# Three attention layers on one core: the order of the first projections, the queue of the next layer's weights, and the order of GpSimd's norm

## The chip, the cores and the metric

One core of a Trainium2 chip runs the whole program. The metric is the device time in microseconds (us); of three runs of the kernel before the median is 2946.81 us (2944.68 to 2946.95).

## The reference, cut to what matters

x has 32 sequences of 128 positions and 512 features. Four layers follow each other, each added to x. The change touches the first three, and the preparation in front of them.

```python
def _L0(x, cond, ...):     # attention, 16 heads of 32 features
    q, k, v = x @ Wqkv.T + bqkv
    attn = softmax(q @ k.T / sqrt(32))
    coh = sigmoid(tanh(concat(x, cond) @ Wc1.T + bc1) @ Wc2.T + bc2)
    mod = attn * coh
    mod = mod / (mod.sum(-1) + 1e-8)
    out = ((1 - 0.21) * mod + 0.21 * fa) @ v      # fa: one row of weights per sequence
    return out @ Wout.T + bout

def _L1(x, mask, cond, ...):
    attn = softmax(where(mask, -inf, q @ k.T * scale))
    out = (attn @ v) @ Wo.T
    return out / rms(out) * rms_scale * (1 + sc) + shift

def _L2(x, t, ...):
    x = x + attention(g1 * x / rms(x) + b1)
    return x + swiglu(g2 * x / rms(x) + b2)       # hidden width 2048

x = x + _L0(x); x = x + _L1(x); x = x + _L2(x); x = x + _L3(x)
```

## The kernel before, in words

The program has three phases, with a barrier of all engines between them: `prepare` (small vectors, and the first weights), `attention` (the attention of three layers), and `gated_mlp`. The change is in the first two.

**Exact products.** Every matrix product in fp32 is made of three passes: an operand is split into a high part (a copy in fp32r by ScalarE, L104, L1013) and a low part (the difference, by VectorE or GpSimd, L109, L1218, L1334). `mm3` then multiplies high by high, high by low and low by high. So before a weight or x can be used it must be loaded, made high, and made low. `Splitter` does that for a list of loads through a few staging tiles: a load waits until the low part of the load that last used its tile is done.

**The start.** `prepare` splits the whole tiles of k's and q's weights of layer 0 (L104 on ScalarE, L109 on VectorE) at its end, and loads the first x and the two halves of c's weights ahead. `attention` then begins with the split of x (`high_x(0)`, `low_x(0)`), and splits the halves of c, v and o. A prologue projects the first group in the order c, v, k, q (c is the projection inside the tanh).

**Bodies.** There are 48 bodies, 16 for each layer; a body handles a group of two sequences. In it are eight units (u = 0 to 7, four heads of one sequence). A unit goes: scores on TensorE (L797), maximum and difference on VectorE (L1129, L1133), exponential on ScalarE (L964), high part on ScalarE (L959), low part on VectorE (`low_probs`, L1137, both inputs in SBUF), a transposition by DMA (`turn_probs`, L652, issued by SyncE), and the weighing of the values on TensorE (`weigh_values`, L813). Between them TensorE makes the projections of the next group (L746 to L748 in two PSUM banks `bank_a`), whose results ScalarE and VectorE read (L947 or L949, L1122), and turns the outputs (L845). `iterate` runs every layer's first body and last three written out, and the twelve between as a loop. Each engine does its own instructions strictly in the order of the code; `pieces_of` sets in which of twelve slots of a body each half of a projection falls.

**Queues.** SyncE issues every transfer: eight transposes per body, and between them a store of the last group's result, loads of residual and x, in some bodies a piece of the weights of later layers (loaded, split and stored in DRAM as `split_h`, `split_l`). At the borders of the layers, `swap` loads the split weights of the next layer back (L684, `new_weight`, 16 transfers of 512 KB per border): four at the end of body 14 (30), eight in body 15 (31), one behind each unit's transposition, and four in and behind the last units of body 16 (32). It waits for the last use of the tile that is written over. The order on SyncE is:

```python
for u in range(UNITS):
    turn_probs(i, u)
    if u == 0 and piece_of(i) is not None:
        load_piece(piece_of(i))
    swap(i, u)
```

**GpSimd.** Values are split into three bf16 parts: `first_values` on ScalarE (L993), `rest_of_values` on GpSimd (L1341), `second_values` on ScalarE (L997), `third_values` on GpSimd (L1345). In layer 2 the norm of x two groups ahead ends on GpSimd too (`norm_end`, eight operations, L1358), behind everything else of the body, when VectorE has scaled x (L1201). In layer 1 `norm_add` (L1211, eight operations of VectorE with two inputs in SBUF) adds the normed output.

**The query mask.** In layer 1, `normalise` multiplies the reciprocal sums (128x8) by `any_key` (L1151) and then the weighed values by the result (L1159).

Of the kernel before, what the change touches and what calls it, by code (L numbers as in the profile page):

```python
# [115 lines left out]
def prepare(nc, hold, k, a, weights, ahead):  # L116

    with ExitStack() as ctx:
# [35 lines left out]
        ws = Splitter(nc, hold, "prep", weights, [sb(f"stage{n}", [P, CH * E]) for n in range(2)])  # L154
# [13 lines left out]
        def _(sp):  # L168
# [7 lines left out]
            for dst, src in ahead:  # L176
                sp.dma_start(dst, src).then_inc(ahead_loaded, 16)
            sp.wait_ge(ahead_loaded, 16 * len(ahead))
# [48 lines left out]
        def _(act):  # L227
# [13 lines left out]
            for n in range(len(weights)):  # L241
                ws.high(act, n)

# [112 lines left out]
def attention(nc, hold, k, x_in, x_out, wh, wl, a, split_h, split_l, hh, hl, xin, spare, stored):  # L356
# [5 lines left out]
    with ExitStack() as ctx:  # L362
# [35 lines left out]
        with ExitStack() as first_layer:  # L398
# [106 lines left out]
        def a_turn(p, fill):  # L505
# [6 lines left out]
            place = 1 if kind == "o" else 2 if kind == "c" else 3 + c - early if kind == "v" else 0 if m == 1 else 2 + c + early  # L512
# [84 lines left out]
        def z_turn(i, j):  # L597

            return 2 * (4 * i + j) if lay(i) < 2 else 4 * i + j + 4 * 2 * G
# [20 lines left out]
        def _(sp):  # L620
# [42 lines left out]
            for n in range(ws.staged, FIRST):  # L663
# [17 lines left out]
            def new_weight(layer, n, m, part):  # L681
                p = len(PIECES) * (layer - 1) + PIECES.index((n, m))
                t, w = ((split_h, wh), (split_l, wl))[part]
                sp.dma_start(f32(columns(w[n], m)), t[p].rearrange("p (c e) -> p c e", c=CH)).then_inc(new_weights[n, m], 16)  # L684

            def last_use(layer, kind, m):
                bk, _ = a_turn(G * layer - 1, (kind, m))
                sp.wait_ge(a_full[bk], a_done(G * layer - 1, (kind, m)))

            def swap(i, u):  # L690

                for layer in (1, 2):
                    at = i - G * layer if isinstance(i, int) else None
                    if at == -2 and u == UNITS:
                        sp.wait_ge(piece_stored, 32 * len(PIECES) * layer)
                        for n in "kq":
                            last_use(layer, n, 0)
                            for part in range(2):
                                new_weight(layer, n, 0, part)
                    if at == -1 and u < 4:  # L700
                        if u == 0:
                            last_use(layer, "v", 1)
                        new_weight(layer, "v", u // 2, u % 2)
                    if at == -1 and 4 <= u < UNITS:
                        if u == 4:
                            last_use(layer, "q", 1)
                        new_weight(layer, "kq"[u // 2 - 2], 1, u % 2)
                    if at == 0 and u >= UNITS - 2:
                        if u == UNITS - 2:
                            last_use(layer, "o", 1)  # L710
                        for m, part in ([(0, u - UNITS + 2)] if u < UNITS else [(1, 0), (1, 1)]):
                            new_weight(layer, "o", m, part)

# [616 lines left out]
        def _(pool):  # L1330
# [38 lines left out]
            def body(i):  # L1369
# [10 lines left out]
                if pre(i):  # L1380
                    norm_end(i + 2)
# [529 lines left out]
```

## Time and profile before

| | |
|---|---|
| Median of three runs | 2946.81 us |
| Time of the profiled execution | 2946.95 us |
| Its span | 2945.2 us |
| TensorE busy | 2832.9 us, 96% |
| VectorE busy | 2077.9 us, 71% |
| ScalarE busy | 1386.7 us, 47% |
| GpSimd busy | 672.8 us, 23% |
| Preparation and prologue | until about 70 us |
| Layers 0, 1, 2 | about 70 to 720, to 1300, to 1856 us |

The span runs from the first instruction to the last; the time has a little around it. Busy time counts no waiting on semaphores, but an instruction that stands inside an engine counts as busy. The row of a timeline gives start, duration, engine, line, and in brackets how long the engine was idle before it and what ended that. "PEclk" is the clock granted to TensorE: 1.00 is its high level (2.4 GHz), 0.50 its low one (1.2 GHz).

### The profile page before, as it was taken

The numbers are of one execution on the slowest core, as the hardware profiler recorded it, in microseconds if no ns is written. First come the engines' busy times: TensorE is split into PE (matmuls) and PEld (weight loads), VectorE is DVE, ScalarE is ACT, GpSimd is POOL, SyncE is SP. The second block draws the span as 40 slices with busy tenths as digits, with TensorE's granted clock in tenths as the row PEclk, the third lists the DMA queues.
The fourth block names the chain that finished last, engine by engine and source line by source line (L and its number), as shares of the span: only waits on it lengthen the run. The fifth ranks groups of instructions, "written<-read, shape, count | busy, mean of one in ns | idle before, by whom it ended". The sixth has DMA issues, their size and how long they took to land. (4 is left out here: it accounts for less than half of the span.)

```text
span 2945.2 us, 69390 instructions
## 1 busy us (share of the span) xinstructions
PE 2832.9 (96%) x26999; PEld 2488.1 (84%) x26999; DVE 2077.9 (71%) x3640; ACT 1386.7 (47%) x2254; POOL 672.8 (23%) x563
## 2 busy tenths in 40 slices
PE   6999999998999999988999998999999999999997
PEld 5899999998899999888888887788888888888886
DVE  5777777786799999978888888644444465555554
ACT  3555555554566666656666666322222232222221
POOL 1222222221111121133233322222222221111112
PEclk8999999999999999999999999999999999999999
DMA  3554544457544443575434445321122230111101
GB/s 141 105 133 117 134 131 136 128 122 187 133 112 105 110 111 100 126 176 135 109 103 115 106 114 128 129 69 60 57 71 84 90 98 29 58 44 51 48 29 43
DMA packets 514586, 300.44 MB, mean 102 GB/s; under 512 B 411776, under 2 KB 484608, under 8 KB 513952
## 3 DMA queue, kind: packets, MB, share of 16 engines
q1 hardware_dynamic: 514464, 298.76, 37.9%
q8 instruction: 83, 1.36, 0.2%
q14 instruction: 39, 0.32, 0.0%
HBM read 139.31 MB, written 58.72 MB: 67 GB/s over the span
## 5 line engine op out<-in xcount | busy, mean ns | idle before, releaser
L746 PE MATMUL att_bank_a<-keep_hh,keep_wgateh 128*128 128x256 f32 x1536 | 449.3, 293 | 0.9 <-ACT att_af L915 0.9
L964 ACT ACTIVATE att_shifted<-att_shifted,keep_lift 128x512 f32<-128x512 f32 x384 | 276.2, 719 | 341.2 <-DVE att_shifted L1133 341.2
L747 PE MATMUL att_bank_a<-keep_hh,keep_wgatel 128*128 128x256 f32 x1536 | 435.3, 283 | 0.0
L748 PE MATMUL att_bank_a<-keep_hl,keep_wgateh 128*128 128x256 f32 x1536 | 435.1, 283 | 0.0
L1730 DVE TENSOR_TENSOR mlp_act_t<-mlp_bank_u,mlp_sg 128x512 f32<-128x512 f32 x128 | 88.4, 690 | 453.5 <-ACT mlp_sg L1636 449.8
L1636 ACT ACTIVATE mlp_sg<-mlp_bank_g 128x512 f32<-128x512 f32 x128 | 76.7, 599 | 628.9 <-PE mlp_bank_u L1560 628.9
L1779 POOL TENSOR_TENSOR mlp_al<-mlp_act_t,mlp_ah 128x512 fp32r<-128x512 f32 x128 | 174.7, 1365 | 863.0 <-ACT mlp_ah L1642 863.0
L1137 DVE TENSOR_TENSOR att_pq<-att_shifted,att_pq 128x512 f16<-128x512 f32 x384 | 331.2, 865 | 45.2 <-ACT att_pq L959 42.6
L746 PEld LDWEIGHTS att_bank_a<-keep_hh,keep_wgateh 128*128 128x128 f32 x1536 | 294.6, 192 | 4.4 <-ACT att_af L915 1.1
L747 PEld LDWEIGHTS att_bank_a<-keep_hh,keep_wgatel 128*128 128x128 f32 x1536 | 295.1, 192 | 0.1
L748 PEld LDWEIGHTS att_bank_a<-keep_hl,keep_wgateh 128*128 128x128 f32 x1536 | 295.0, 192 | 0.0
L1129 DVE TENSOR_REDUCE att_top<-att_bank_s 128x4 f32<-128x512 f32 x384 | 261.2, 680 | 32.7 <-PE att_bank_s L797 32.6
L1133 DVE TENSOR_TENSOR att_shifted<-att_bank_s,att_top 128x512 f32<-128x512 f32 x384 | 265.5, 691 | 16.4
L959 ACT ACTIVATE att_pq<-att_shifted 128x512 f16<-128x512 f32 x384 | 242.4, 631 | 66.6 <-DMA att_pt<-att_pq 47.2
L813 PEld LDWEIGHTS att_bank_o<-keep_v,att_pt 128*128 128x128 f16 x7680 | 206.4, 96 | 59.4 <-DVE att_of L1159 19.5
L813 PE MATMUL att_bank_o<-keep_v,att_pt 128*128 128x34 bf16 x7680 | 226.9, 178 | 28.7 <-DMA att_pt<-att_pq 17.5
L746 PE MATMUL att_bank_a<-att_oth,keep_wuph 128*128 128x256 f32 x768 | 225.9, 294 | 20.4 <-DVE att_kl L1122 17.5
L747 PE MATMUL att_bank_a<-att_oth,keep_wupl 128*128 128x256 f32 x768 | 217.2, 283 | 0.0
L748 PE MATMUL att_bank_a<-att_otl,keep_wuph 128*128 128x256 f32 x768 | 217.0, 283 | 0.0
L1560 PE MATMUL mlp_bank_y<-mlp_al,mlp_woh 128*128 128x512 f32 x512 | 203.5, 398 | 0.0
L1558 PE MATMUL mlp_bank_y<-mlp_ah,mlp_woh 128*128 128x512 f32 x512 | 202.2, 395 | 1.4 <-POOL mlp_al L1779 1.4
L1559 PE MATMUL mlp_bank_y<-mlp_ah,mlp_wol 128*128 128x512 f32 x512 | 202.9, 396 | 0.0
(268 smaller groups left out, 7123.0 us busy)
## 6 DMA issues: line engine op xcount, KB each, us to landing
resid<-att_xres SPq DMA_DIRECT2D x47, 512.0 KB, 3.0
keep_xin<-resid SPq DMA_DIRECT2D x33, 512.0 KB, 3.8
mlp_res<-resid SPq DMA_DIRECT2D x32, 512.0 KB, 4.5
att_xres<-resid SPq DMA_DIRECT2D x31, 512.0 KB, 4.1
mlp_xf<-resid SPq DMA_DIRECT2D x30, 512.0 KB, 4.5
keep_xin<-in_x SPq DMA_DIRECT2D x16, 512.0 KB, 4.2
att_xres<-in_x SPq DMA_DIRECT2D x16, 512.0 KB, 3.9
keep_spare<-in_w_next SPq DMA_DIRECT2D x16, 512.0 KB, 3.8
```

The source lines that it names most:

```text
L746: nc.tensor.matmul(out, w_h, x_h, start=first, stop=False)
L747: nc.tensor.matmul(out, w_l, x_h, start=False, stop=False)
L748: return nc.tensor.matmul(out, w_h, x_l, start=False, stop=last)
L813: mm = nc.tensor.matmul(bank_o[:, o:o + VW], pt[:, u % TURNED, part, h, :], v[:, b, 4 * c + h, :], start=(n == 0), stop=(n == len(passes) ...
L959: nc.scalar.activation(pq[:, u % 2, 0], shifted[:, u % 2], ACT.Copy).then_inc(p_high, 1)
L964: nc.scalar.activation(shifted[:, u % 2], shifted[:, u % 2], ACT.Exp, bias=k["lift"][:, 0:1], scale=SCALE).then_inc(exp_done, 1)
L1129: nc.vector.reduce_max(top[:, u % 2, :], src, AX_X).then_inc(top_ready, 1)
L1133: nc.vector.tensor_tensor(shifted[:, u % 2], src, bcast_last(top[:, u % 2, :], P), ALU.subtract).then_inc(shift_done, 1)
L1137: nc.vector.tensor_tensor(pq[:, u % 2, 1], shifted[:, u % 2], pq[:, u % 2, 0], ALU.subtract).then_inc(p_low, 1)
L1558: nc.tensor.matmul(out, w[0], x_h, start=first, stop=False)
L1559: nc.tensor.matmul(out, w[1], x_h, start=False, stop=False)
L1560: return nc.tensor.matmul(out, w[0], x_l, start=False, stop=last)
```

## The change

1. `prepare` splits only v's weights (one load, one staging tile). It also splits the first x: high part on ScalarE behind v's, low part on GpSimd (a wait for `x_loaded`, one for `x_high`). `attention` no longer does either.
2. The prologue projects v, then c, k, q. Eight half-tile loads (c, k, q, o) go through the three staging tiles; their splits stand at given slots of the prologue (`SPLIT_AT`), among the reads of the results, the last (o) before q's read.
3. `new_weight`, `last_use` and `swap` move from SyncE to ScalarE, unchanged in themselves; ScalarE calls `swap` for two units at the end of each pair of units.
4. SyncE issues two transposes, then what else belongs to the pair: the piece's load stands behind unit 1 (before: 0), the store behind unit 5 (before: 4), the residual and x loads where they were.
5. GpSimd does `norm_end` in the next body, between `rest_of_values` and `third_values` (before: last in the body before). The final one stands behind all bodies.
6. In layer 1 the factor `any_key` is part of the operation at L1159; L1151 and a wait go.

```diff
-        ws = Splitter(nc, hold, "prep", weights, [sb(f"stage{n}", [P, CH * E]) for n in range(2)])
+        ws = Splitter(nc, hold, "prep", weights, [sb("stage", [P, CH * E])])
...
         @block.gpsimd
...
+            high, low = x_split
+            pool.wait_ge(x_high, 1)
+            nc.gpsimd.tensor_tensor(low, ahead[0][0], f32(high), ALU.subtract)
...
             for n in range(len(weights)):
                 ws.high(act, n)
+            act.wait_ge(x_loaded, 16)
+            nc.scalar.activation(x_split[0], ahead[0][0], ACT.Copy).then_inc(x_high, 1)
...
-        FIRST = 6
+        SPLIT_AT = {0: (0, 1), 7: (2, 3), 8: (4, 5), 10: (6, 7)}
...
-                 for n in "cvo" for m, part in enumerate(halves)]
+                 for n in "ckqo" for m, part in enumerate(halves)]
...
-            ahead = values + keys if values_first(i) else keys + values
-            return [("k", 1), ("q", 1), ("o", 0), ("o", 1)] + ([("c", 0), ("c", 1)] if lay(i + 1) == 0 else []) + ahead
+            hidden = [("c", 0), ("c", 1)] if lay(i + 1) == 0 else []
+            return [("k", 1), ("q", 1), ("o", 0), ("o", 1)] + (values + hidden + keys if values_first(i) else hidden + keys + values)
...
             def body(i):
-                for u in range(UNITS):
+                for u in range(0, UNITS, 2):
                     turn_probs(i, u)
+                    turn_probs(i, u + 1)
                     if u == 0 and piece_of(i) is not None:
                         load_piece(piece_of(i))
-                    swap(i, u)
-                    if u == 1 and post(i):
+                    if u == 0 and post(i):
                         load_residual(i - 1)
                     if u == 4 and positive(i) and not post(i):
                         store(i - 1)
-                    if u == 5 and has(i, 2) and lay(i + 2) < 2:
+                    if u == 4 and has(i, 2) and lay(i + 2) < 2:
                         load(i + 2)
...
-                swap(i, UNITS)
...
         @block.scalar
...
+            def new_weight(layer, n, m, part):
+                p = len(PIECES) * (layer - 1) + PIECES.index((n, m))
+                t, w = ((split_h, wh), (split_l, wl))[part]
+                act.dma_start(f32(columns(w[n], m)), t[p].rearrange("p (c e) -> p c e", c=CH)).then_inc(new_weights[n, m], 16)
...
             act.wait_ge(eps_set, 1)
-            high_x(0)
             for s, pieces in enumerate(pieces_of(-1)):
-                if s < FIRST and s % 2 == 0:
-                    for n in (s, s + 1):
-                        ws.high(act, n)
+                for n in SPLIT_AT.get(s, ()):
+                    ws.high(act, n)
...
+                    if s < UNITS:
+                        swap(i, s)
+                        swap(i, s + 1)
+                swap(i, UNITS)
...
-                if lay(i) == 1:
-                    nc.vector.tensor_scalar(r, r, k["any_key"][:, 0:1], None, ALU.mult).then_inc(rz_step, 1)
...
-                nc.vector.tensor_tensor(dst, src[:, :, :, 0:HD], scale, ALU.mult).then_inc(o_free, 1)
+                if lay(i) == 1:
+                    nc.vector.scalar_tensor_tensor(out=dst, in0=src[:, :, :, 0:HD], scalar=k["any_key"][:, 0:1], in1=scale,
+                                                   op0=ALU.mult, op1=ALU.mult).then_inc(o_free, 1)
+                else:
+                    nc.vector.tensor_tensor(dst, src[:, :, :, 0:HD], scale, ALU.mult).then_inc(o_free, 1)
...
             def body(i):
                 for b in range(NB):
                     rest_of_values(i, b)
+                if positive(i) and pre(i - 1):
+                    norm_end(i + 1)
                 for b in range(NB):
                     third_values(i, b)
...
-                if pre(i):
-                    norm_end(i + 2)
 
             iterate(pool, body)
+            norm_end(ALL + 1)
             low_x(ALL + 1)
...
-            early = [(a["L0_" + n], flat3(wh[n]), flat3(wl[n])) for n in "kq"]
+            early = [(a["L0_v"], flat3(wh["v"]), flat3(wl["v"]))]
...
-            phase(prepare, a, early, ahead)
+            phase(prepare, a, early, ahead, (hh[:, :, 0:T], hl[:, :, 0:T]))
```

## Rows read from the trace of the kernel before

**Rows 1.** The page, part 1: busy time, share of the span, instructions

```profile
PE 2832.9 (96%) x26999; PEld 2488.1 (84%) x26999; DVE 2077.9 (71%) x3640; ACT 1386.7 (47%) x2254; POOL 672.8 (23%) x563
```

**Rows 2.** TensorE's waits, total, times, longest: 60-690, 695-800, 1184-1375, 1375-1753 us

```profile
PE att_bank_s L797 <- DVE att_shifted L1133: 4.9, 1, 4.9
...
PE att_bank_o L813 <- DMA att_pt<-att_pq: 9.5, 6, 4.4
...
PE att_bank_o L813 <- DMA att_pt<-att_pq: 5.3, 4, 1.9
...
PE att_bank_a L746 <- DVE att_kl L1122: 10.8, 12, 0.9
```

**Rows 3.** Layer 1: busy PE, PEld, DVE, ACT, POOL, then clock, DMA, GB/s

```profile
801.00:1184.00 383.00, 381.47 (x4999) 348.61 (x4998) 352.41 (x635) 257.64 (x402) 80.08 (x57) 1.00 0.42 107
```

**Rows 4.** The timeline of the start

```profile
32.50 4.48 DVE L109 TENSOR_TENSOR keep_wgatel<-prep_stage,keep_wgateh 128x2048 fp32r<-128x2048 f32 x2
...
38.01 1.06 ACT L1013 ACTIVATE keep_hh<-keep_xin 128x1024 fp32r<-128x1024 f32 x1 [6.71 <-DVE att_eps L1224]
...
42.73 0.58 PE L746 MATMUL att_bank_a<-keep_hh,att_wch 128*128 128x256 f32 x1 [11.85 <-DVE att_wcl L109]
...
54.08 0.50 PE L746 MATMUL att_bank_a<-keep_wuph,keep_hh 128*128 128x512 f32 x1 [3.14 <-ACT att_tf L933]
...
70.95 0.69 DVE L1129 TENSOR_REDUCE att_top<-att_bank_s 128x4 f32<-128x512 f32 x1 [1.96 <-PE att_bank_s L797]
```

**Rows 5.** The start in windows, columns as in rows 3

```profile
44.00:46.00 2.00, 2.00 (x11) 2.00 (x11) 0.00 (x0) 0.64 (x1) 0.00 (x0) 0.50 0.92 330
...
54.00:60.00 6.00, 5.92 (x19) 4.73 (x20) 0.94 (x2) 2.32 (x7) 2.56 (x2) 0.72 0.00 0
...
64.00:66.00 2.00, 2.00 (x19) 2.00 (x18) 0.76 (x2) 0.84 (x2) 0.00 (x0) 1.00 0.00 0
```

**Rows 6.** Borders: timeline, windows, and lines 652 (1240-1310 us) and 684 (680-724)

```profile
703.41 1.72 SPq L652 DMA_TRANSPOSE att_pt<-att_pq  x1
...
708.93 0.75 PE L813 MATMUL att_bank_o<-keep_v,att_pt 128*128 128x34 bf16 x20 [4.38 <-DMA att_pt<-att_pq]
...
706.00:708.00 2.00, 0.00 (x0) 0.00 (x0) 0.00 (x0) 0.00 (x0) 0.00 (x0) 0.67 1.13 278
...
680.00:723.00 43.00, 36.94 (x446) 33.56 (x445) 26.65 (x58) 17.20 (x31) 4.87 (x4) 0.92 0.71 185
...
L652 SPq DMA_TRANSPOSE att_pt<-att_pq x11: 1232/1819/3964, 1242.6 to 1306.2; - x11
...
DMA to landing us min/median/max: 2.7/4.7/8.1
...
L684 SPq DMA_DIRECT2D keep_wgateh<-split_h x2: 583/584/585, 701.6 to 708.4; - x2
```

**Rows 7.** The start of a body of layer 2: timeline, and the body's window

```profile
1544.24 3.45 POOL L1358 TENSOR_SCALAR att_xf<-att_xf,att_gt,att_bt 128x128 f32<-128x128 f32 x8 [22.33 <-DVE att_xf L1201]
1547.66 2.22 POOL L1341 TENSOR_TENSOR att_vr<-att_vf,keep_v 128x512 f32<-128x512 f32 x2
...
1547.58 2.84 DVE L1137 TENSOR_TENSOR att_pq<-att_shifted,att_pq 128x512 f16<-128x512 f32 x1 [0.22 <-ACT att_pq L959]
...
1551.75 0.38 PE L746 MATMUL att_bank_a<-att_oth,keep_wuph 128*128 128x256 f32 x1 [0.94 <-DVE att_kl L1122]
...
1517.30:1550.80 33.50, 32.38 (x438) 29.73 (x434) 29.50 (x47) 21.77 (x36) 10.65 (x14) 1.00 0.42 110
```

**Rows 8.** Line 1211 beside the norm's end (second border), and alone (layer 1)

```profile
1298.97 4.21 POOL L1358 TENSOR_SCALAR att_xf<-att_xf,att_gt,att_bt 128x128 f32<-128x128 f32 x8 [9.64 <-DVE att_xf L1201]
...
1299.28 2.30 DVE L1211 SCALAR_TENSOR_TENSOR att_xres<-att_af,att_gt,att_xres 128x128 f32<-128x128 f32 x8
...
868.04 2.18 DVE L1211 SCALAR_TENSOR_TENSOR att_xres<-att_af,att_gt,att_xres 128x128 f32<-128x128 f32 x8
```

**Rows 9.** The costliest groups of VectorE: busy, mean ns, idle before

```profile
L1151 DVE TENSOR_SCALAR att_rz<-att_rz,keep_any_key 128x8 f32<-128x8 f32 x64 | 33.0, 515 | 2.3
```

More of the change, by code:

```diff
@@ L113, in flat3, with prepare @@
     return t[:].rearrange("p c e -> p (c e)")
-def prepare(nc, hold, k, a, weights, ahead):
+def prepare(nc, hold, k, a, weights, ahead, x_split):
     with ExitStack() as ctx:
@@ L175, in _ @@
                 ws.load(sp, n)
-            for dst, src in ahead:
+            x, x_dram = ahead[0]
+            sp.dma_start(x, x_dram).then_inc(x_loaded, 16)
+            for dst, src in ahead[1:]:
                 sp.dma_start(dst, src).then_inc(ahead_loaded, 16)
-            sp.wait_ge(ahead_loaded, 16 * len(ahead))
+            sp.wait_ge(ahead_loaded, 16 * (len(ahead) - 1))
         @block.gpsimd
@@ L662, in _ @@
             sp.sem_inc(x_loaded, 16)
-            for n in range(ws.staged, FIRST):
+            sp.sem_inc(x_high, 1)
+            sp.sem_inc(x_split, 1)
+            for n in range(ws.staged, len(loads)):
                 if n == 4:
@@ L1019, in high_piece, with last_use, swap @@
                 nc.scalar.activation(part_h[:], spare[0][:], ACT.Copy).then_inc(piece_high, 1)
+            def new_weight(layer, n, m, part):
+                p = len(PIECES) * (layer - 1) + PIECES.index((n, m))
+                t, w = ((split_h, wh), (split_l, wl))[part]
+                act.dma_start(f32(columns(w[n], m)), t[p].rearrange("p (c e) -> p c e", c=CH)).then_inc(new_weights[n, m], 16)
+            def last_use(layer, kind, m):
+                bk, _ = a_turn(G * layer - 1, (kind, m))
+                act.wait_ge(a_full[bk], a_done(G * layer - 1, (kind, m)))
+            def swap(i, u):
+                for layer in (1, 2):
+                    at = i - G * layer if isinstance(i, int) else None
+                    if at == -2 and u == UNITS:
+                        act.wait_ge(piece_stored, 32 * len(PIECES) * layer)
+                        for n in "kq":
+                            last_use(layer, n, 0)
+                            for part in range(2):
+                                new_weight(layer, n, 0, part)
+                    if at == -1 and u < 4:
+                        if u == 0:
+                            last_use(layer, "v", 1)
+                        new_weight(layer, "v", u // 2, u % 2)
+                    if at == -1 and 4 <= u < UNITS:
+                        if u == 4:
+                            last_use(layer, "q", 1)
+                        new_weight(layer, "kq"[u // 2 - 2], 1, u % 2)
+                    if at == 0 and u >= UNITS - 2:
+                        if u == UNITS - 2:
+                            last_use(layer, "o", 1)
+                        for m, part in ([(0, u - UNITS + 2)] if u < UNITS else [(1, 0), (1, 1)]):
+                            new_weight(layer, "o", m, part)
             act.wait_ge(eps_set, 1)
-            high_x(0)
             for s, pieces in enumerate(pieces_of(-1)):
-                if s < FIRST and s % 2 == 0:
-                    for n in (s, s + 1):
-                        ws.high(act, n)
+                for n in SPLIT_AT.get(s, ()):
+                    ws.high(act, n)
                 for fill, part in pieces:
@@ L1224, in _ @@
             nc.vector.memset(eps[:], 1e-6).then_inc(eps_set, 1)
-            low_x(0)
             nc.vector.tensor_copy(tb[:], k["tanh_bias"][:, :, 0:NB]).then_inc(tb_ready, 1)
             for s, pieces in enumerate(pieces_of(-1)):
-                if s < FIRST and s % 2 == 0:
-                    for n in (s, s + 1):
-                        ws.low(dve, n)
+                for n in SPLIT_AT.get(s, ()):
+                    ws.low(dve, n)
                 for fill, part in pieces:
```

45 lines of the change are left out of this document (8 added, 37 removed).

## The prediction

> **What bounds the kernel now.** I read the page first: TensorE is busy 96% of the span, no other engine over 71% [rows 1]. So an edit pays only where it takes away an idle stretch of TensorE, or a stretch at its half clock. The second view is TensorE's waits, stage by stage [rows 2]: after the start there is one wait of 4.9 us in the 630 us of layer 0, and in the middle of layer 1 TensorE is busy 381.5 of 383 us [rows 3]. Nothing is to be won there. What is left lies in four places: the start, the two borders of the layers, and one wait of some 0.9 us in every body of layer 2.
>
> The sum is made against the profiled execution, 2946.95 us (span 2945.2); the median of the runs shown is 2946.81, the same for this purpose. About 0.2% (5.9 us) can be told from no change here.
>
> **The change, part by part.**
>
> *1. The start.* The timeline shows the chain [rows 4]. In the preparation VectorE splits two full weight tiles (k, q) in 4.48 us, 2.24 each, until 36.98. ScalarE's next work starts at 38.01, 1.03 later: the border of the phases. Then the first x is split and c's two halves, and only at 42.73 does TensorE start, having waited 11.85 us. The change leaves one tile (v) in the preparation, moves x's split there (its low part from VectorE to GpSimd), and lets TensorE start with v. Preparation ends at 32.50 + 2.24 = 34.74, and I add 0.5 us because GpSimd now works beside VectorE at its end (below); with 1.03 and 0.1 for the start, TensorE begins at 36.4 instead of 42.73: 6.3 us. Second, before, TensorE stood 3.14 us at 54.08 for ScalarE's read of the c result, which in ScalarE's order stands behind the splits of all o halves. In the new order the k, q and o halves are split between the reads of results. Behind that wait TensorE's clock fell to its low level again: its mean over 54 to 60 is 0.72, so (1 - 0.72) x 6 / 0.5 = 3.4 us were low [rows 5]. What a low stretch costs, products of 256 columns show: 11 in 2 us at the low level, 19 at the high one, so a low us loses 1 - 11/19 = 0.42 us, the stretch 1.4. From TensorE's first projection to the first read of scores there are 70.95 - 42.73 = 28.2 us; without gap and low stretch 23.7, so scores arrive at 60.1. **10.8 us saved.** Bounds: 6.3 if a late k or q half brings the gap back (three staging tiles now serve eight loads), 12 if GpSimd costs VectorE nothing. What follows (body 0 with its 4.9 us wait) is moved as it is. In all of TensorE's later work in this layer the order is unchanged.
>
> *2. The queue of the borders.* 32 transfers of 512 KB (16 per border) leave SyncE's queue for ScalarE's. Before, they stand in one queue with the transposes of the probabilities. At the first border a transposition is issued at 703.41, takes SyncE 1.72 us instead of the 1.23 of the quickest, and at 708.93 TensorE has waited 4.38 us for a transposition, while the DMA engines' share is 1.13, that is full, and the clock falls [rows 6]. In all TensorE waits 9.5 us for transposes at the first border and 5.3 at the second [rows 2]; there the median transposition lands after 4.7 us, the quickest after 2.7, and one issue took 3.96 [rows 6]. The mean clock of 0.92 over 43 us at the first border means 6.9 low us, which cost 2.9; I take as much for the second. So at most 9.5 + 5.3 + 5.8 = 21 us hang on it. Against it: each issue (0.58 us on SyncE, [rows 6]) now stands in ScalarE's stream, where exponentials and high parts queue behind it, then VectorE's low parts, the transposes, and TensorE's weighing of values. Body 15 gets eight, two behind each pair, 8 x 0.58 = 4.7 us. ScalarE is busy 17.2 of 43 us there [rows 6], so the cover exists; if it is gone, all 32 cost 32 x 0.6 = 19 us. No row shows two queues at once. Between -21 and +19 I take -7, a third of the gain: the bytes are the same and the engines full just when TensorE waits, yet a transposition no longer stands wholly behind a weight. The waits that ScalarE takes over (last uses, stored pieces) ask for what it has read or what is long done.
>
> The Trainium skill (DMA: Bandwidth & Descriptors, "Issuing engines are not separate DMA queues") says that transfers of all issuing engines interleave on the same 16 engines and a second issuer saves only issue time. By that rule this term would be about 0; no run so far shows it for this kernel.
>
> *3. SyncE's order.* Transposes go in pairs, and the store, the load and the piece follow the pair. Three transfers per body keep their place; the store and the piece move behind one transposition, which then goes 0.5 us earlier. In the steady bodies TensorE waits for none. In the last body it may give 0.5 us; I count 0.
>
> *4. The end of the norm on GpSimd.* This is the wait in layer 2. In each body [rows 7] GpSimd does the eight operations of the norm (1544.24, 3.45 us), and behind them the values' rests (1547.66, 2.22 us for two). VectorE's low part of the probabilities starts at 1547.58 and takes 2.84 us, and ends half a us after both rests: it stood for them. The low part of k comes behind it, and TensorE, which needs its bank, waits 0.94 us. The change puts the rests first. They stand behind the norm without a gap, so they are ready before it ends; I take them as ready where it starts, at 1544.1, and they end at 1546.3, ahead of the low part. Then the norm's eight run beside the low part. What that costs is in the second border: eight VectorE operations with two inputs in SBUF took 2.30 us beside the norm's eight and 2.18 us alone [rows 8], and the norm stretched to 4.21. So of the low part's 2.84 us some 2 go and it ends near 1548.6; k's low part is then bound by ScalarE's high output and ends about 0.9 us earlier, and the 0.94 vanishes. The waits add up to 10.8 us in 12 bodies [rows 2], with 0.9 in one more. The body's other limits: TensorE is busy 32.4 of 33.5 us, VectorE 29.5, the standing counted in [rows 7]. GpSimd's third parts of the values and the split of x come behind the norm instead of before it; GpSimd's own work per body stays as it is, and the norm's new end (1546.3 + 4.2 = 1550.5 at most) is 0.6 us behind the rests' old one, 1549.9. **10 us saved**, bounds 0 (the low part waits for all eight) and 12.
>
> *5. The query mask.* In layer 1 the small product (64 times, mean 515 ns [rows 9]) is folded into the following one, an operation of the same size. That is 33 us less of VectorE, but TensorE does not wait there [rows 3]: 0, at most 1 us at the second border.
>
> Sum: 10.8 + 7 + 0 + 10 + 0 = 27.8 us. 2946.95 - 27.8 = **2919 us**.
>
> **Rivals.** *A, the queue change gives nothing* (full engines interleave, as the skill's rule says): 2926. For it speaks the share of 1.13; against it SyncE's long issues. It has 0.25. *B, the borders give all*: the transposes pass the weights, the low stretches go too, 14 us more: 2905. 0.13. *C, the norm still holds VectorE*: if GpSimd's chain of eight lets VectorE in as little as the two rests did, the low part waits until 1549.9 as before, and layer 2 keeps its 0.94: 2929. Against it the 2.30 beside 2.18. The Trainium skill (SBUF — State Buffer, "Who interferes with whom") has GpSimd and such a VectorE operation block each other for a whole instruction, whoever was first; by that the wait would be one of eight, 0.43 us, and C false. 0.15. *D, slower than before*: an issue on ScalarE waits for the queue as SyncE's did, 3.96 us at the longest. Each pair's stop is then 7.9 us against some 4 us of ScalarE's idle time (26 us of body 15's 43, in its six steps); each of the 16 pairs loses 4 us, 64 us, against 20 won elsewhere: about 2990. It decides where an issue costs over 2.6 us: then 16 x (2 x 2.6 - 4) = 20. Against it, the weights' own issues took SyncE 0.58 us. 0.04. The rest, 0.43, is my forecast.
>
> **How the numbers follow.** The likeliest is 2919. Two of A, C and a late start together give about 2936; B gives 2905. The range 2904 to 2935 leaves out D, the worst of A with C, and the best of B. Faster by over 0.2%: everything but D and part of an unforeseen loss, 0.94. Within 0.2%: 0.03. Slower: 0.03.
>
> **What would show it.** Start: TensorE's first projection near 36.4, the first read of scores near 60. Layer 2: the low part at a body's start takes under 1.4 us, no wait on k's low part, a body of about 32.6 us. Borders: waits of TensorE for transposes under 10 us together, ScalarE's issues near 0.6 us. Wrong would be: the gap before c's or q's projection in the prologue again, the rests' stretch of VectorE now on its additions of the norm at the second border (there 2.3 could grow to 4), or waits for exponentials in bodies 15 and 31.

## The result, and the profile after

The changed kernel takes 2925.72 us at the median of five runs (2923.85 to 2931.92), against 2946.81 before (five runs by now): the ratio is 0.9937, interval 0.9925 to 0.9949. That is 21 us less, where 2919 was forecast; the range held it. By the interval of the ratio it is 15 to 22 us less. The profiled execution has a span of 2923.9 us.

The page, part 1, and two queues of its part 3 (packets, megabytes, share of the 16 engines):

```profile
PE 2830.9 (97%) x26999; PEld 2490.7 (85%) x26999; DVE 2026.3 (69%) x3576; ACT 1389.2 (48%) x2255; POOL 682.3 (23%) x564
...
q1 hardware_dynamic: 497712, 281.99, 35.5%
q10 hardware_dynamic: 16896, 16.78, 2.0%
```

TensorE's work is the same; VectorE has 52 us and 64 instructions less [rows 1]. The second queue is ScalarE's, with the 32 weights.

TensorE's waits, in three stretches that answer to those of before (60 to 670, 670 to 795 and 1160 to 1375 us; for each the line that stands in [rows 2]). From 1360 to 1740 us there is none.

```profile
PE att_bank_s L773 <- DVE att_shifted L1144: 4.9, 1, 4.9
...
PE att_bank_o L789 <- DMA att_pt<-att_pq: 14.7, 3, 6.4
...
PE att_bank_o L789 <- DMA att_pt<-att_pq: 4.0, 4, 1.4
```

The wait of body 0 is unchanged. The wait for transposes at the first border has grown from 9.5 to 14.7 us. The twelve waits on k's low part in layer 2, 10.8 us, are gone.

The start in the timeline, and in windows (columns as in rows 3):

```profile
30.45 2.34 POOL L190 TENSOR_TENSOR keep_hl<-keep_xin,keep_hh 128x1024 fp32r<-128x1024 f32 x1 [26.73 <-ACT keep_hh L250]
...
31.73 1.53 DVE L357 TENSOR_SCALAR keep_gain<-prep_sc,keep_pack 128x32 f32<-128x32 f32 x4
...
33.28 2.27 DVE L109 TENSOR_TENSOR keep_wupl<-prep_stage,keep_wuph 128x2048 fp32r<-128x2048 f32 x1
...
36.62 0.80 PE L722 MATMUL att_bank_a<-keep_wuph,keep_hh 128*128 128x512 f32 x1 [5.83 <-SPq L672]
```

```profile
44.00:46.00 2.00, 2.00 (x18) 1.96 (x17) 1.61 (x2) 1.06 (x1) 0.00 (x0) 1.00 0.54 203
54.00:60.00 6.00, 6.00 (x68) 5.79 (x67) 4.28 (x7) 3.51 (x6) 2.21 (x2) 1.00 0.06 23
```

TensorE starts at 36.62 in place of 42.73, there is no gap and no low clock from 44 to 60 any more [rows 4, 5], and the first scores are read at 59.60.

The first border in the timeline, SyncE, ScalarE and TensorE, then the window of bodies 15 to 17.

```profile
688.61 4.62 SPq L660 DMA_TRANSPOSE att_pt<-att_pq  x2
...
687.96 0.55 ACTq L1000 DMA_DIRECT2D keep_wgateh<-split_h  x1
688.54 0.65 ACTq L1000 DMA_DIRECT2D keep_wgatel<-split_l  x1
...
697.76 0.63 ACT L935 ACTIVATE att_pq<-att_shifted 128x512 f16<-128x512 f32 x1 [5.07 <-DMA att_pt<-att_pq]
...
697.81 1.29 PE L789 MATMUL att_bank_o<-keep_v,att_pt 128*128 128x34 bf16 x40 [5.14 <-DMA att_pt<-att_pq]
```

```profile
665.79:794.67 128.88, 110.33 (x1363) 100.41 (x1364) 87.08 (x162) 60.95 (x98) 16.85 (x13) 0.92 0.68 158
```

ScalarE issues two weights at 687.96, SyncE a pair of transposes 0.65 us later. The pair is what ScalarE (which needs its buffer) and TensorE wait for until 697.8. The bodies 15 to 17 take 128.9 us; before they took 124.3.

A body of layer 2, GpSimd and VectorE at its start, and its window:

```profile
1530.04 2.21 POOL L1351 TENSOR_TENSOR att_vr<-att_vf,keep_v 128x512 f32<-128x512 f32 x2 [21.04 <-ACT keep_v L969]
1532.22 4.04 POOL L1368 TENSOR_SCALAR att_xf<-att_xf,att_gt,att_bt 128x128 f32<-128x128 f32 x8
...
1533.59 0.69 DVE L1148 TENSOR_TENSOR att_pq<-att_shifted,att_pq 128x512 f16<-128x512 f32 x1 [0.21 <-ACT att_pq L935]
```

```profile
1530.56:1562.98 32.42, 32.33 (x436) 29.71 (x436) 27.35 (x47) 21.76 (x35) 11.23 (x14) 1.00 0.42 113
```

The rests stand first, the low part takes 0.69 us beside the norm in place of 2.84, and the body 32.42 in place of 33.50 [rows 7].

The product with the mask is folded into this one (64 times, mean 484 ns), where before the plain one cost 424 and the small one 515 [rows 9]:

```profile
L1168 DVE SCALAR_TENSOR_TENSOR att_of<-att_bank_o,keep_any_key,att_rz 128x256 f32<-128x256 f32 x64 | 31.0, 484 | 4.7
```

To see where the time goes I take, from the timeline of every kernel, the time at which the first scores of a body are read (L1140 here, L1129 before). The first line is in us from the span's start, the others are differences from it. Body 15 is the last of layer 0, body 18 is past the first border, 18 to 28 the steady bodies of layer 1, 34 past the second border, 47 the last.

| kernel | 0 | 15 | 18 | 28 | 34 | 47 |
|---|---|---|---|---|---|---|
| before | 70.95 | 677.23 | 801.52 | 1144.71 | 1377.30 | 1812.53 |
| after | -11.4 | -11.4 | -6.9 | -9.1 | -8.9 | -20.6 |
| q_sp | -12.3 | -12.7 | -19.2 | -21.5 | -21.6 | -34.1 |
| q_sp_old | -12.3 | -12.1 | -14.9 | -17.1 | -17.6 | -29.6 |
| issue_only | -11.4 | -11.6 | -17.1 | -19.5 | -19.7 | -32.8 |
| act_in_before | -1.8 | -1.7 | +5.5 | +5.4 | +11.8 | +12.7 |
| act_each_unit | -13.0 | -13.3 | -8.7 | -10.8 | -11.4 | -23.7 |
| act_old_order | -11.2 | -10.5 | -6.5 | -8.6 | -9.2 | -20.8 |
| norm_back | -11.9 | -11.2 | -5.4 | -7.6 | -6.6 | -5.9 |
| norm_only | -0.8 | -0.6 | 0.0 | 0.0 | +4.0 | -7.2 |
| mask_apart | -13.2 | -13.5 | -7.9 | -8.0 | -1.5 | -13.7 |
| q_sp_mask | -11.5 | -11.4 | -15.8 | -15.8 | -13.0 | -24.7 |

Kernels with the same start differ there by up to 2.2 us from trace to trace; differences between two columns of one row are firmer. So after: 11.4 us at the start, a loss of 4.6 at the first border, 2.2 in layer 1, nothing over the second border, 11.8 in layer 2. The forecast had 10.8, then a gain of 7 over both borders, 0, and 10. Inside a border the first read of a single body's scores can move by 4 us and leave the sum as it was, so only sums over a whole border are used.

### The profile page after: what moved, and what is told of

It reads as the page before. It is cut to its first block and busy times, and to the rows that moved or that the text cites. A ratio compares the mean times of both kernels' runs of the same rounds, so it can differ in the third digit from the quotient of the medians.

```text
span 2923.9 us, 69283 instructions
## 1 busy us (share of the span) xinstructions
PE 2830.9 (97%) x26999; PEld 2490.7 (85%) x26999; DVE 2026.3 (69%) x3576; ACT 1389.2 (48%) x2255; POOL 682.3 (23%) x564
## 5 line engine op out<-in xcount | busy, mean ns | idle before, releaser
L1148 DVE TENSOR_TENSOR att_pq<-att_shifted,att_pq 128x512 f16<-128x512 f32 x384 | 309.9, 807 | 39.4 <-ACT att_pq L935 35.6
L1140 DVE TENSOR_REDUCE att_top<-att_bank_s 128x4 f32<-128x512 f32 x384 | 261.5, 681 | 41.5 <-PE att_bank_s L773 41.4
L1351 POOL TENSOR_TENSOR att_vr<-att_vf,keep_v 128x512 f32<-128x512 f32 x96 | 106.7, 1134 | 674.9 <-ACT keep_v L969 674.9
L722 PE MATMUL att_bank_a<-att_oth,keep_wuph 128*128 128x256 f32 x768 | 227.7, 296 | 12.4 <-DVE att_kl L1133 7.5
```

What stands on the lines that cost most here:

```text
L722: nc.tensor.matmul(out, w_h, x_h, start=first, stop=False)
L1140: nc.vector.reduce_max(top[:, u % 2, :], src, AX_X).then_inc(top_ready, 1)
L1148: nc.vector.tensor_tensor(pq[:, u % 2, 1], shifted[:, u % 2], pq[:, u % 2, 0], ALU.subtract).then_inc(p_low, 1)
```

## The experiments

Every run was timed beside executions of the kernel before, in four batches whose medians for it are 2943.5, 2946.1, 2944.9 and 2947.3 us (2946.8 beside the changed kernel). So two medians of different batches can differ by some 3 us for no reason of the kernel. The ratios don't carry this.

**q_sp: the weights stay on SyncE's queue, all else as changed.**

```diff
-act.dma_start(f32(columns(w[n], m)), ...)
+sp.dma_start(f32(columns(w[n], m)), ...)
 ...
 turn_probs(i, u)
 turn_probs(i, u + 1)
+swap(i, u)
+swap(i, u + 1)
```

> The changed kernel with the 32 weight transfers back on SyncE's queue, two behind each pair of transposes. Theory S (sharing: weights on a second queue run in between the packets of a transposition and stretch it): the median transposition at the first border lands after about 3.5 us instead of 6.0, TensorE's waits for transposes there fall from 14.7 us to about 8, the first border no longer gives 4.5 us back, and the time is about 2919 (2925.7 - 6.5). Rival O (the loss comes from SyncE's new order in pairs): the waits and the time stay, 2925. Rival I (the issue on ScalarE costs): as S in time, but the landing of transposes stays near 6 us.

Measured: 2914.34 us (2910.98 to 2914.91), ratio to before 0.9901, interval 0.9884 to 0.9917. It is 11 us faster than the changed kernel by the medians (10.6 by the ratios), about what theory S says in kind and nearly twice in size (it had 2919). Rival O is out, and rival I by the landings below. The first border's three bodies take 117.9 us in place of 128.9. How the transposes land, for their line between 660 and 765 us, first after, then q_sp; then q_sp's waits from 680 to 765 and its window of the border:

```profile
DMA to landing us min/median/max: 2.7/6.0/10.0
```

```profile
DMA to landing us min/median/max: 2.7/2.8/7.9
```

```profile
PE att_bank_o L825 <- DMA att_pt<-att_pq: 7.5, 3, 5.5
```

```profile
664.49:782.36 117.87, 106.66 (x1363) 97.50 (x1364) 86.86 (x162) 60.56 (x98) 16.77 (x13) 0.96 0.64 159
```

A transposition takes 6.0 us to land with the weights on a second queue and 2.8 with them on its own, and the weights themselves 7.0 in place of 5.4. TensorE waits 14.7 - 7.5 = 7.2 us more for transposes. A clock of 0.92 over 128.9 us against 0.96 over 117.9 is 20.6 - 9.4 = 11.2 us more at the low level, which at the 0.42 us lost in each cost 4.7 by estimate. The windows give the split without it: of the 11.0 us TensorE is busy 3.7 longer (110.33 against 106.66) and idle 7.3 longer.

**q_sp_old: the same with SyncE's old order too** (for each unit its transposition, then its weight, loads between as before).

> As q_sp, and SyncE's order unit by unit as in the kernel before. S: about the same as q_sp, 2919 within 2 us; layer 1's body keeps its 34.10 us if that gain is the mask's. O: 2919 while q_sp is at 2925. If the pairs are what shortened layer 1's body, it is 34.32 us here.

Measured: 2918.79 us (2917.45 to 2919.95), ratio 0.9916, interval 0.9900 to 0.9933: 4.4 us more than q_sp, 4.3 - 0.6 = 3.7 of them at the first border. The pairs do gain, where the weights share the queue. Layer 1's body keeps its 34.10 us, so its 0.22 us are not the pairs'. Here, in body 15, every transposition but the first stands right behind a weight of its own queue, and the median landing is 3.4 us: more than q_sp's 2.8, and far from the 6.0 beside a second queue.

**act_in_before: the kernel before with this one edit**, the weights issued by ScalarE behind each pair.

> The kernel before with only the 32 weight transfers moved to ScalarE's queue. S: slower at the first border by about 4 to 5 us (waits for transposes from 9.5 to some 14 us), about 2 at the second: 2952 to 2954. O: no change, 2947. My forecast's term would be 2940.

Measured: 2958.59 us (2953.94 to 2959.52), ratio 1.0045, interval 1.0028 to 1.0062. Alone, the headline of the change makes the kernel 13 to 15 us slower: 7.2 at the first border and 6.4 from body 28 to 34, at the second. Theory S had the sign and about half of the size (4 to 5, and 2). The transposes land after 5.2 us at the first border (4.3 before):

```profile
DMA to landing us min/median/max: 2.7/5.2/9.5
```

**issue_only: is it ScalarE's time?** The weights go on SyncE's queue as in q_sp, and ScalarE issues 32 transfers of 8 KB at the places where it issued weights.

```diff
+act.dma_start(junk[:, tiny[0]], d[:, :, 0:4]).then_inc(junk_done, 16)
```

> q_sp, and ScalarE issues 32 transfers of 8 KB (64 bytes by partition, from the same tensors) at the places where it issued the weights. It leaves nothing of the computation out. S: within 1 us of q_sp, landing of transposes as there. I (issue time in ScalarE's stream): slower than q_sp by about 5 us, as the changed kernel.

Measured: 2913.28 us (2912.42 to 2918.69), ratio 0.9902, interval 0.9886 to 0.9919. The same as q_sp, and the median landing at the first border is 3.0 us. Issuing 32 transfers costs ScalarE's chain nothing that shows; the loss is in the large transfers. (The 8 KB ones carry next to no traffic, so this separates the issue from the bytes.)

**act_each_unit: are the bursts of two to blame?** The queue is ScalarE's, one weight behind each unit.

```diff
 high_probs(i, u)
+swap(i, u)
 ...
-if s < UNITS:
-    swap(i, s)
-    swap(i, s + 1)
```

> The changed kernel with one weight issued by ScalarE behind each unit's high part, in place of two behind each pair; the queue is ScalarE's still. Theory (the second queue stretches the transposes, wherever its transfers are issued): the first border stays 8 us or more longer than with SyncE's queue (body 15 to body 18 takes 129 us, 123 with SyncE's) and the time is about 2925. Rival: the bursts of two weights ahead of a pair of transposes are the cause; then it comes near the version with SyncE's queue, 2914 to 2918.

Measured: 2925.17 us (2922.92 to 2927.54), ratio 0.9934, interval 0.9918 to 0.9951. The border's bodies take 128.9 us, as in the changed kernel. So a burst of two is not needed for the loss, nor does it matter that one of the weights now goes out 2 us ahead of the pair (666.13, the pair's first at 668.13). (The 123 us in the expectation should have been q_sp's 117.9.)

**extra_sp and extra_act: the two queues where nothing waits for the large transfers.** q_sp has no weights in bodies 45 and 46. Both kernels add sixteen transfers of 512 KB there, which nobody reads.

```diff
+if i in (ALL - 3, ALL - 2) and u < UNITS:
+    ENG.dma_start(split[p], f32(columns(w["o"], m))).then_inc(extra_done, 16)
```

> The changed kernel with its border weights on SyncE's queue (2914.3 us), and in bodies 45 and 46, where no weights are fetched, sixteen transfers of 512 KB more (o's parts written back to scratch in DRAM), issued by SyncE, two behind each pair of transposes. They have no reader; their weight is their traffic alone. Both theories: a transposition stands behind at most two of them, each 1.5 to 3 us, and bodies 45 and 46 grow little, by 0 to 4 us together: 2914 to 2918.

> As the run beside it, with the same sixteen transfers issued by ScalarE at the same places of its own stream. Theory: transfers of a second queue run in between the transposes' packets and stretch the transposes: their median landing in bodies 45 and 46 rises by 1 us or more above that of SyncE's, TensorE waits for them, and the two bodies take 4 to 8 us longer than with SyncE's: 2919 to 2925. Rival: the loss at the borders came from when ScalarE reaches its issues and from what the weights wait for, not from the second queue; then both runs are within 1 us of each other, since nothing waits for these transfers.

Measured: 2918.40 us (2917.09 to 2921.40) on SyncE's queue, 2922.66 (2919.67 to 2926.01) on ScalarE's. From the first scores of body 45 to those of 47 the traces have 66.1 us without extras, 71.1 with them on SyncE's queue, 76.8 on ScalarE's. The issues' median time to landing in these bodies, without extras, on SyncE's, on ScalarE's queue:

```profile
att_pt<-att_pq SPq DMA_TRANSPOSE x16, 2.8
```

```profile
split_h<-keep_wuph SPq DMA_DIRECT2D x8, 512.0 KB, 3.4
...
att_pt<-att_pq SPq DMA_TRANSPOSE x16, 4.1
```

```profile
q1 hardware_dynamic: 17760, 7.34, 41.4%
q10 hardware_dynamic: 8448, 8.39, 35.0%
...
split_h<-keep_wuph ACTq DMA_DIRECT2D x8, 512.0 KB, 4.0
...
att_pt<-att_pq SPq DMA_TRANSPOSE x16, 5.1
```

The same bytes cost 5.0 us on the transposes' own queue and 10.7 on the second. No weight is waited for here and nobody reads the extras, so no late weight can be the cause: what shows is the transposes' lateness (2.8, 4.1, 5.1 us) and TensorE's waits for them, 1.9 us with extra_sp and 5.0 with extra_act in these bodies. The expectation had 0 to 4 us for the first, which is 5.0, and 4 to 8 us between the two; it is 5.7 in the traces and 4.3 in the medians. The last fence's queues (packets, MB, share) show what meets: the first moves 7.34 MB in 17760 packets, mostly the transposes' small ones, the second 8.39 MB in 8448.

One thing does differ besides the queue: when the large transfers are issued. extra_sp first, then extra_act, at the first pair of body 45:

```profile
1715.65 5.08 SPq L661 DMA_TRANSPOSE att_pt<-att_pq  x2
1720.79 0.67 SPq L731 DMA_DIRECT2D split_h<-keep_wuph  x1
```

```profile
1712.26 19.17 SPq L661 DMA_TRANSPOSE att_pt<-att_pq  x6
1712.27 0.67 ACTq L1040 DMA_DIRECT2D split_h<-keep_wuph  x1
```

SyncE issues them behind both transposes of a pair, ScalarE at the time of the first. It is the same at the border: in body 15 of q_sp the weights follow the start of a pair by 4.1 to 6.7 us, in the changed kernel they are issued within 0.7 us of it. No run holds ScalarE's issues back until the pair is out. So it is shown that large transfers on ScalarE's queue, issued when its own work comes to them, delay the transposes. How much of that is the queue and how much the moment is open.

**act_old_order: the changed kernel with SyncE's old order.**

> The changed kernel with SyncE's old order: the x load, the residual's load and the last bodies' loads stand between the transposes of a pair again; the weights stay on ScalarE's queue. With the weights on SyncE the pairs gained 4.4 us, nearly all at the first border. If the pairs gain because a transposition then stands behind fewer transfers of its own queue, they gain as much or less where the weights have left that queue: 2926 to 2930. Rival: the order gains nothing by itself and only its place among SyncE's weights did: 2925.7 within 1 us.

Measured: 2927.42 us (2925.74 to 2928.72), ratio 0.9935, interval 0.9921 to 0.9948: 1.7 us more in the medians, whose ranges overlap, and at body 47 the two traces stand at -20.8 and -20.6. The 2927.4 lies in the theory's range and 0.7 us beyond the rival's, but the ratios (0.9935 and 0.9937) and the traces tell no difference. The pairs are worth 4 us with the weights in their queue, and nothing that can be told once these have left it.

**norm_back: the changed kernel with the norm's end last on GpSimd again.**

```diff
-if positive(i) and pre(i - 1):
-    norm_end(i + 1)
 ...
+if pre(i):
+    norm_end(i + 2)
```

> The changed kernel with the eight operations of the norm's end again the last of GpSimd's body, as before the change; all else stays. If their place is what shortened layer 2: its bodies take 33.5 us again in place of 32.4, VectorE's low part at their start takes 2.8 us again, TensorE waits some 0.9 us on k's low part in each of twelve bodies, layers 0 and 1 stay within 1 us of the changed kernel, and the time is 12 us above the changed kernel's 2925.7: about 2938. Rival: layer 2 gained by SyncE's pairs or by the lighter borders behind it; then its bodies stay at 32.4 us and the time at 2926.

Measured: 2938.65 us (2929.89 to 2942.56), ratio 0.9972, interval 0.9962 to 0.9983: 12.9 us more than after by the medians, 10.3 by the ratios (ten runs, which scatter more than others do). In the traces 12.4 of it lies between bodies 34 and 47. Its waits in layer 2 (1370.7 to 1806) and a body's window and low part are those of before again:

```profile
PE att_bank_a L722 <- DVE att_kl L1133: 11.0, 12, 1.0
```

```profile
1507.72 2.84 DVE L1148 TENSOR_TENSOR att_pq<-att_shifted,att_pq 128x512 f16<-128x512 f32 x1 [0.21 <-ACT att_pq L935]
```

```profile
1504.69:1538.19 33.50, 32.37 (x436) 29.71 (x435) 29.49 (x47) 21.77 (x35) 10.64 (x14) 1.00 0.41 110
```

**norm_only: the kernel before with this edit alone.**

> The kernel before the change with one part of it alone: the eight operations of the norm's end go behind the values' rests on GpSimd. If their place alone is what shortens layer 2: its bodies take 32.4 us in place of 33.5, layers 0 and 1 do not move, and the time is 12 to 15 us below the kernel before: ratio 0.995. Rival: it needs the rest of the change (SyncE's pairs, the fold) to show: bodies of 33.0 us or more and a ratio above 0.997.

Measured: 2938.12 us (2936.13 to 2941.26), ratio 0.9975, interval 0.9965 to 0.9984, 7 us less and half of what was expected. Layer 2 is as foreseen (bodies of 32.4 us, 11.1 from body 34 to 47), but 3.9 us are lost between bodies 28 and 34. In body 31 VectorE and GpSimd do this:

```profile
1263.77 5.18 DVE L1137 TENSOR_TENSOR att_pq<-att_shifted,att_pq 128x512 f16<-128x512 f32 x1
...
1259.88 3.99 POOL L1358 TENSOR_SCALAR att_xf<-att_xf,att_gt,att_bt 128x128 f32<-128x128 f32 x8
1263.85 2.20 POOL L1345 TENSOR_TENSOR keep_v<-att_vr,keep_v 128x512 bf16<-128x512 f32 x2
1266.01 2.38 POOL L1334 TENSOR_TENSOR keep_hl<-att_xf,keep_hh 128x1024 fp32r<-128x1024 f32 x1
```

The second low part of the body now meets the third parts and x's split, which the norm has pushed behind it: three long two-input operations of GpSimd with no gap between, and VectorE stands through all of them, 5.18 us for an operation of 0.69. The changed kernel has the same 5.18 in body 31, act_old_order and issue_only 5.17; q_sp has no low part over 2.41 us there.

```profile
1240.66 5.17 DVE L1190 TENSOR_TENSOR att_pq<-att_shifted,att_pq 128x512 f16<-128x512 f32 x1
```

That it costs the 3.9 us is tempting and not shown. issue_only, whose row this is, has it and takes 132.4 us from body 28 to 34, and so does q_sp, which has not; the changed kernel takes 132.8. These have the folded mask, and norm_only has not. The run that would settle it, norm_only with the fold, was not made. And at the end of that body the rests stretch the norm's additions of VectorE, in the changed kernel:

```profile
1288.90 2.39 POOL L1351 TENSOR_TENSOR att_vr<-att_vf,keep_v 128x512 f32<-128x512 f32 x2 [9.96 <-ACT keep_v L969]
1289.09 3.76 DVE L1223 SCALAR_TENSOR_TENSOR att_xres<-att_af,att_gt,att_xres 128x128 f32<-128x128 f32 x7
```

3.76 us for seven, 4.02 with the one ahead of them, where before eight took 2.30 [rows 8]. Nothing shows that it costs time: q_sp has 4.00 there and loses nothing over this border, and norm_only, which loses, has 2.19.

**mask_apart: the changed kernel with the mask a product of its own in layer 1.**

```diff
+if lay(i) == 1:
+    nc.vector.tensor_scalar(r, r, k["any_key"][:, 0:1], None, ALU.mult)
```

> The changed kernel with the query mask of layer 1 again a small product of its own, 64 of them. If the fold is what takes 0.22 us off each body of layer 1: body 18 to body 28 takes 343.2 us again in place of 341.0, and the time is 3 to 4 us above the changed kernel: about 2929. Rival: the 0.22 us come from the order in which SyncE issues the transposes and the loads (it was there with the old order too, which speaks against it), or from the norm's new place: then no change, 2926.

Measured: 2933.89 us (2932.86 to 2936.37), ratio 0.9958, interval 0.9942 to 0.9975: 8.2 us more than after, twice what was expected. Layer 1's bodies take 34.32 us again (2.2 us from body 18 to 28), and from 28 to 34 it loses 6.5 us where after loses 0.2. Seven steady bodies, 21 to 27, of before and of after show the mechanism (columns as in rows 3):

```profile
904.47:1144.71 240.24, 239.27 (x3152) 218.35 (x3151) 220.88 (x400) 162.11 (x253) 49.53 (x35) 1.00 0.42 107
```

```profile
896.95:1135.65 238.70, 238.70 (x3151) 218.82 (x3152) 210.59 (x373) 162.49 (x253) 49.53 (x35) 1.00 0.42 108
```

TensorE stood 0.14 us in each of seven bodies, too short to be listed as a wait, and stands no more. The other 0.08 of the 0.22 us are busy time of TensorE (239.27 against 238.70), for which no row gives the reason. VectorE is busy 10.3 us less, 1.5 in each body. (The fence of before is shown because its stretch is not among the rows ahead.)

**q_sp_mask: the mask apart again, with the weights on SyncE's queue.**

> The changed kernel with its border weights on SyncE's queue (2914.3 us) and the query mask again a small product of its own. With ScalarE's queue the same edit cost 8 us: 2.7 in the bodies of layer 1 and 5.5 at the second border. If the 5.5 us are what VectorE's slack saves only where late transposes crowd its work (the second queue), then here only the 0.22 us of each body of layer 1 come back: 2917. Rival: the fold is worth 8 us with either queue: 2922.

Measured: 2922.18 us (2921.21 to 2924.88), ratio 0.9924, interval 0.9907 to 0.9940: 7.8 us more than q_sp. The expectation, that the fold pays at the borders only together with the second queue, is wrong, and the rival right: the fold is worth 8 us with either queue. Here they lie at the first border (2.1 us over bodies 15 to 17, of which the last two are layer 1's), in the steady bodies (2.3) and at the second border (2.9 from 28 to 34).

## Why the prediction was right or wrong

The total came out 7 us above the forecast, but two terms of the sum had missed by more and partly cancelled. What each edit brings in the changed kernel, from the median with it undone: norm 12.9, fold 8.2, SyncE's order 0 to 1.7, the queue a loss of 11.4; the start, from the trace, 11.4. That is a gain of 21 to 23 us, and 21.1 was measured. By the ratios, which leave out what differs between batches, it is norm 10.3, fold 6.2, the queue a loss of 10.6, and with the start a gain of 17, where the ratio of the changed kernel says 18.6. So each term is known to some 2 or 3 us. The start was not undone in a run by itself. That the total came so near is in part luck: a term 18 us too high stands against one 8 us and one up to 3 us too low.

*The start (10.8 forecast): right.* 11.4 us between these two traces, 9.4 to 13.4 between any two traces with the old and the new start. The preparation's last product of VectorE starts at 33.28, 0.8 later than before, by GpSimd's split of x: the four small operations at L357 took 1.53 us where they had taken 0.68. It is the 0.5 put in for it, and a little more. TensorE began at 36.62 (36.4 forecast), without gap and low clock, and scores came at 59.60 (60.1).

*The queue of the borders (a gain of 7 forecast): wrong, in sign.* The step that failed is "yet a transposition no longer stands wholly behind a weight". It may be true and it is no gain. In one queue, with the weights behind a pair, half of q_sp's transposes at the border land within 0.1 us of the quickest; that the two weights are mostly through when the next pair comes is my reading of this. With two queues, transposes and weights both land later (6.0 for 2.8, 7.0 for 5.4 us), as they would if they ran side by side. That this is a sharing of the engines, packet by packet, is again a reading; what the runs show is the landings. Part of it may be the moment of the issue and not the queue, as said at extra_act. With the second queue the median landing went from 2.8 to 6.0 us, TensorE's wait from 7.5 to 14.7 and the clock from 0.96 to 0.92. The other half of the working held: an issue takes ScalarE 0.55 to 0.65 us and hides. At the second border the same 16 transfers cost the changed kernel 0.4 us against q_sp (132.8 and 132.4 from body 28 to 34) and act_in_before 6.4 against the kernel before; why the first is so little is open. TensorE's waits for transposes at both borders, forecast under 10 us together, are 14.7 + 4.0. The bounds, -21 to +19, held the +11; the likeliest value, a third of the gain, had no row behind it. Rival A had the right doubt and too mild a price; that its 2926 is the time measured is chance, since it rests on a queue that costs nothing and a mask that gives nothing.

The rule of the Trainium skill (DMA: Bandwidth & Descriptors, "Issuing engines are not separate DMA queues"), by which the term would be 0, was nearer than mine. That the transfers interleave fits the landings. That a second issuer changes nothing but the time of issuing did not hold here: the same sixteen large transfers cost 5.7 us more where ScalarE issued them.

*SyncE's order (0): right*, where it stands, as act_old_order shows. It is worth 4 us beside weights in the same queue, which the forecast did not ask.

*The norm on GpSimd (10): right in mechanism and place, the size was 10 to 13 undone and 7 alone.* The low part takes 0.69 us (under 1.4 forecast), the body 32.42 (32.6), the twelve waits went. Alone it also brings its 11.1 us in layer 2, and loses 3.9 at the second border, for a cause that is open. Not seen in the steady body's rows was what the norm pushes behind it: at the second border third parts and x's split land on a low part, 5.18 us. The forecast had listed the stretch of the norm's additions as a thing that would be wrong, and it came (4.02 us). Neither cost anything that shows where the mask is folded. The Trainium skill (SBUF — State Buffer, "Who interferes with whom") says that an operation of VectorE with two inputs in SBUF and one of GpSimd that reads it block one another. The traces agree as to the norm, where GpSimd gave way (3.45 to 4.04 us) and VectorE did not. Three long operations in a row are not covered by waiting for one: in body 31 VectorE stood for all three. Rival C, the whole chain of eight holding VectorE, is out by the 0.69.

*The mask (0, at most 1): wrong, 6 to 8 us.* The step that failed is "TensorE does not wait there". Two things were missed. TensorE's 1.5 us of idle time in 383 [rows 3] are 0.14 in every body, below what the waits list, and 0.22 us of the body came back. And the two borders, where VectorE's chain is late, have layer 1's bodies on one side each. There the fold is worth 2.1 us at the first border and 2.9 at the second with SyncE's queue, and 1.1 and 6.3 with ScalarE's. The profile of before had it: of TensorE's waits from 1184 to 1375 us these, 13.5 us, are ended by VectorE, against 5.3 by transposes.

```profile
PE att_bank_a L746 <- DVE att_kl L1122: 6.8, 5, 1.8
...
PE att_bank_o L813 <- DVE att_of L1159: 3.4, 3, 1.9
PE att_bank_b L853 <- DVE att_quarter L1179: 3.3, 2, 1.7
```

*Rivals.* B (the borders give all, 2905) is out for the changed kernel. B had 21 us over the borders. Even in q_sp the first border gives 6.4 us and the second nothing, and of the 6.4 the fold is 2.1 and the pairs 3.7. D (ScalarE's issues wait) is out by their 0.55 to 0.65 us, with one of 1.23.

## What to carry to other kernels

When small, urgent transfers share the 16 engines with large ones that nobody is waiting for, try first to keep both on one queue, with the large ones right behind the urgent: on a second queue, issued without regard to the urgent ones, they cost this kernel 11 us over its first border. (At its second they cost 0.4, and a second queue whose transfers follow the urgent ones was not tried.) Try each part of a change by itself, and each part undone as well: the headline of this one cost 11 us in a kernel that gained 21, and the part that was costed at nothing gave 6 to 8. Idle time spread as 0.14 us over every body, and bodies at the ends of a layer where the same engine is late, both counted here for an edit that shortens that engine's work, even though the middle of the layer shows TensorE at 99.6%.

## What the runs showed of the hardware that was not expected

- Two issuing engines' large and small transfers in flight together: sixteen transfers of 512 KB cost 5.0 us on the transposes' queue, issued behind each pair, and 10.7 on the other, issued beside it, with the transposes' median landing at 4.1 and 5.1 us (2.8 without).
- VectorE's low part (two inputs in SBUF, 0.69 us alone) took 5.17 or 5.18 us where it began 0.07 to 0.10 us ahead of three operations of GpSimd in a row (2.20 for two and 2.38 us), in four kernels. 0.15 us behind the first of them, in the body of layer 2, it took 1.53. What decides whether VectorE gets in between two of them was not tried.
- VectorE's four small operations at L357 (inputs in SBUF), 0.68 us alone, took 1.53 us beside GpSimd's split of x.
- Issuing a transfer of 512 KB took ScalarE's queue 0.55 us for the high part and 0.65 for the low.
